# A factorization-machine tower on one core: the order-zero Gram matrices computed in 64x64 tiles, two samples at a time

## What is computed

```
h = e                                  # layer 0
for i, (W, b) in enumerate(layers):    # W0, W1, W2 with 128 outputs each
    nxt = einsum('bjk,bzk,ojz->bok', h, e, W.reshape(O, Hj, 32)) + b
    h, o = nxt[:, :64], nxt[:, 64:]    # the last layer gives all 128 to o
z = sum over k of all the o            # [512, 256]
y = relu(relu([z, dense_ctx] @ W_top1 + b_top1) @ W_top2 + b_top2) @ W_top3
```

## Time and profile before

| | us |
|---|---|
| median of three runs (lowest, highest) | 696.14 (693.29, 696.73) |
| the profiled execution's own time | 695.17 |
| its span, first to last instruction | 693.4 |
| TensorE matmul busy | 652.9 (94%) |
| VectorE busy | 483.7 (70%) |
| ScalarE busy | 215.4 (31%) |
| GpSimd busy | 129.6 (19%) |

### The profile page before, as it was taken

How to read it: one execution, slowest core, us unless ns; L and a number is a source line. 1 busy time by engine, 2 the same in 40 slices (tenths; PEclk the granted TensorE clock), 3 DMA queues, 4 the chain that set the end, 5 groups by cost and what they waited for, 6 DMA issues and landing times.

```text
span 693.4 us, 32990 instructions
## 1 busy us (share of the span) xinstructions
PE 652.9 (94%) x15000; PEld 513.3 (74%) x15000; DVE 483.7 (70%) x488; ACT 215.4 (31%) x354; POOL 129.6 (19%) x137
## 2 busy tenths in 40 slices
PE   5745999999999999999999999999999999999798
PEld 5734767777778777877878787878788887888563
DVE  4238878888888888888888888888888888820000
ACT  2331333333334333433333333333333333331002
POOL 7755134454445444000000000000000000000000
PEclk9976999999999999999999999999999999999889
DMA  5100011111111111000000000000000000020000
GB/s 174 29 19 17 15 20 23 23 24 23 23 23 21 20 20 23 9 10 9 8 8 8 8 8 8 8 8 8 8 8 8 8 8 8 8 70 9 4 1 0
DMA packets 13036, 12.64 MB, mean 18 GB/s; under 512 B 5649, under 2 KB 10305, under 8 KB 12754
## 3 DMA queue, kind: packets, MB, share of 16 engines
q1 hardware_dynamic: 8818, 7.99, 4.5%
q0 software_dynamic: 4192, 4.25, 3.1%
HBM read 8.03 MB, written 0.00 MB: 12 GB/s over the span
## 4 chain that ended last, share of the span: by engine, by line
PE 89%; POOL 5%; issue 3%; DVE 2%; DMA 1%; ACT 0%; ACTq 0%; DVEq 0%; POOLq 0%
PE psX L315 20%; PE psT L369 19%; PE psT L353 8%; PE psT L393 8%; PE psT L379 7%; PE psT L356 5%; PE psX L324 5%; POOL G_sb L219 5%; PE psX L353 4%; PE psX L356 4%; PE psX L443 2%; PE psX L332 1%; DVE PT L692 1%; PE psT L469 1%; PE psX L458 1%
## 5 line engine op out<-in xcount | busy, mean ns | idle before, releaser
L373 PE MATMUL psT<-T_sb,W1d 64*64 64x256 f32 x1024 | 234.3, 379 | 0.0
L369 PE MATMUL psT<-T_sb,W1d 64*64 64x256 f32 x1024 | 234.3, 379 | 0.0
L379 PE MATMUL psT<-T_sb,W1d 64*64 64x256 f32 (+3 forms) x2048 | 205.3, 300 | 0.0
L656 DVE TENSOR_TENSOR prod<-X 128x1024 f32 (+4 forms) x202 | 170.7, 913 | 18.4 <-PE psT L356 18.2
L692 DVE STREAM_TRANSPOSE PT<-prod 128x4608 f32<-128x4608 f32 x32 | 159.0, 4968 | 0.0
L369 PEld LDWEIGHTS psT<-T_sb,W1d 64*64 64x64 f32 x1024 | 131.3, 133 | 29.4 <-issue 17.1
L315 PE MATMUL psX<-PT,W0T 32*64 32x256 f32 x4608 | 137.0, 380 | 10.1 <-DVE PT L692 9.1
L393 PE MATMUL psT<-T_sb,W1d 64*64 64x64 f32 (+2 forms) x1536 | 141.7, 270 | 0.0
L315 PEld LDWEIGHTS psX<-PT,W0T 32*64 32x64 f32 x4608 | 117.2, 133 | 32.1 <-issue 27.1
L373 PEld LDWEIGHTS psT<-T_sb,W1d 64*64 64x64 f32 x1024 | 131.3, 133 | 0.0
L379 PEld LDWEIGHTS psT<-T_sb,W1d 64*64 64x64 f32 x2048 | 123.6, 133 | 0.8
(11 more groups left out here) (74 smaller groups left out, 570.1 us busy)
## 6 DMA issues: line engine op xcount, KB each, us to landing
X<-T_sb SPq DMA_DIRECT2D x64, 64.0 KB, 1.9
G_sb<-in_L_rec_W SPq DMA_DIRECT2D x2, 1024.0 KB, 6.7
E_q<-in_tbl,ids_g POOLq DMA_INDIRECT x96
prod<-in_W_top SPq DMA_DIRECT2D x2, 512.0 KB, 4.2
G_sb<-in_L_rec_W SPq DMA_DIRECT2D x1, 512.0 KB
G_sb<-in_tbl,ids POOLq DMA_INDIRECT x32, 2.4
zb<-in_L_rec_b SPq DMA_DIRECT2D x4, 0.2 KB
ids_g<-in_ids POOLq DMA_DIRECT2D x3, 16.0 KB, 2.0
```

Of the source, the lines that this page charges most:

```text
L369: mm(psT[low, 0, 0:HF * SMP], W1d[low, HF + k, :], cross.rearrange("p v (z y) s -> p v z y s", y=HF)[:, :, :, k, :], start=start, stop=sto ...
L373: mm(psT[high, 0, 0:HF * SMP], W1d[low, k, :], T_flat[low, SMP * row:SMP * (row + HF)], start=start, stop=stop, tile_position=(0, C))
L379: last = mm(out[:, SMP * 4 * a:], W1d[high, HF * v + k, :], T_flat[high, SMP * (row + 4 * a):SMP * (row + HF)], start=start, stop=stop and ...
L656: return tt(out, x[:, :, z0:z0 + nz].unsqueeze(3).broadcast_to(shape), x[:, :, y0:y0 + ny].unsqueeze(2).broadcast_to(shape), ALU.mult)
```

## The change

G0 of two neighbouring tiles is computed by one matmul in a 64x64 tile of the array. `fields` holds, for each pair of tiles, a one, 32 fields of the first, 32 fields of the second, and a one: 66 columns (`GRAM`). 64 of them are the weights, all 66 are moved, so the 64x66 result has the two Gram matrices on its diagonal blocks, the sums beside them, and two cross blocks that nobody reads. There are 8 such matmuls in a step in place of 16.

In `kept` each sample has 34 columns (`NS`), 33 of them written: a sample of an even tile has its ones in column 0, one of an odd tile in column 33, and the fields are columns 1 to 32. The column that is not written is set to zero once at the start. Since where a 32-partition quarter's columns lie depends on the quarter being even or odd, `g0_copy` becomes four copies, one for each quarter of the partitions, each as long in the free dimension as the one before. `z0` and `z2` read `kept` at the shifted columns. `T_BANKS` exchanges the banks of tiles 2 and 3, and `t_matmuls` has its waits in the order that follows from it.

```diff
-NS = NF + 1
+NS = NF + 2
+GRAM = 2 * NF + 2
+ONES = (0, NF + 1)
...
-        fields = sb("fields", [P, 2, TILES, NS])
+        fields = sb("fields", [P, 2, TILES // 2, GRAM])
...
-        T_BANKS = [psT[:, 2:4], psX[:, 0:2], psX[:, 2:4], psT[:, 0:2], psT[:, 2:4], psX[:, 0:2], psT[:, 0:2], psT[:, 2:4]]
+        T_BANKS = [psT[:, 2:4], psX[:, 0:2], psT[:, 0:2], psX[:, 2:4], psT[:, 2:4], psX[:, 0:2], psT[:, 0:2], psT[:, 2:4]]
...
             def g0_matmuls(m, e):
-                for t in range(TILES):
+                for pair in range(TILES // 2):
+                    q, g = pair // 2, pair % 2
                     for h in range(2):
-                        x = fields[C * h:C * h + C, e, t, :]
-                        j, q = t % 4, t // 4
-                        last = mm(psX[Q * j:Q * j + Q, 2 + h, NS * q:NS * (q + 1)], x[:, 0:NF], x,
-                                  start=True, stop=True, tile_position=(C * h, Q * j))
+                        x = fields[C * h:C * h + C, e, pair, :]
+                        last = mm(psX[C * g:C * g + C, 2 + h, GRAM * q:GRAM * (q + 1)], x[:, 1:1 + 2 * NF], x,
+                                  start=True, stop=True, tile_position=(C * h, C * g))
                 last.then_inc(g0_ready, 1)
 
             def t_matmuls(n, e):
                 for t in range(TILES):
                     if t == 2:
+                        pe.wait_ge(g2_copied, n + 1)
+                    if t == 3:
                         pe.wait_ge(g0_evac, n + 1)
-                    if t == 3:
-                        pe.wait_ge(g2_copied, n + 1)
                     if t == 4:
                         pe.wait_ge(t_by_act, NA * n + 1)
-                    if t in (5, 6):
-                        pe.wait_ge(t_by_dve, ND * n + t - 4)
-                    if t == 7:
-                        pe.wait_ge(t_by_act, NA * n + 3)
+                    if t == 5:
+                        pe.wait_ge(t_by_dve, ND * n + 1)
+                    if t in (6, 7):
+                        pe.wait_ge(t_by_act, NA * n + t - 4)
...
-                              kept[:, n0:n0 + STEPS // 2, 4 * NF:4 * NS].rearrange("p n (q h) -> p n q h", h=2),
+                              kept[:, n0:n0 + STEPS // 2, 4 * ONES[j % 2]:4 * ONES[j % 2] + 4]
+                              .rearrange("p n (q h) -> p n q h", h=2),
...
-                c = 4 * y
+                c = 4 * (1 + y)
...
             def g0_copy(m):
                 act.wait_ge(g0_ready, m + 1)
-                copy(kept[:, bass.ds(m, 1), :].rearrange("p n (c q h) -> p (n h) q c", q=2, h=2),
-                     psX[:, 2:4, 0:2 * NS].rearrange("p h (q c) -> p h q c", q=2)).then_inc(g0_evac, 1)
+                for j in range(4):
+                    r, i = slice(Q * j, Q * j + Q), j % 2
+                    last = copy(kept[r, bass.ds(m, 1), 4 * i:4 * (i + NF + 1)].rearrange("p n (c q h) -> p (n h) q c", q=2, h=2),
+                                psX[r, 2:4, 0:2 * GRAM].rearrange("p h (q c) -> p h q c", q=2)[:, :, :, (NF + 1) * i:(NF + 1) * (i + 1)])
+                last.then_inc(g0_evac, 1)
...
+            for c in ONES:
+                nc.vector.memset(kept[:, :, 4 * c:4 * c + 4], 0.0)
             nc.vector.memset(V_T[:, :, :], 0.0).then_inc(zeroed, 1)
-            nc.vector.memset(fields[:, :, :, NF:NS], 1.0)
+            nc.vector.memset(fields[:, :, :, 0:GRAM:GRAM - 1], 1.0)
...
             def x_of(e, first_tile):
-                cp(fields[:, e, :, 0:NF], X_fields[:, bass.ds(first_tile, TILES), :])
+                cp(fields[:, e, :, 1:1 + 2 * NF],
+                   X_fields[:, bass.ds(first_tile, TILES), :].rearrange("p (pair i) f -> p pair (i f)", i=2))
```

## The result

The changed kernel takes 712.56 us (median of four runs, 709.79 to 714.34) against 696.43 for the kernel before (median of four, one run more than in the table ahead), a ratio of 1.0241 (95% interval 1.0205 to 1.0278). It is slower by 16.1 us; the forecast was 713.5. The profiled execution took 711.53, 16.4 more than the one before.

A forecast was written before the change was run, and what follows sets the result against it. TensorE, busy for 94% of the span, was taken as the bound, with ScalarE's copies on the edge of its critical path; 31 x 0.56 = +17.4 on 695.17 gives 712.5, plus 0.97 to the median, 713.5; range 693 to 722.

The forecast's parts named there:

- the middle: ScalarE, start of the first small copy: between 0.62 as now and 0.70, when G2's copy has ended; 0.66 taken.
- The rule on the partitions: ScalarE's four copies: runs whose partitions change don't overlap, so 0.417 each, 1.67 for the four.
- The saving: G0's matmuls on TensorE: 16 record pairs in place of 32 save 0.14 of 0.29, swallowed by the chain over ScalarE.
- The last step: TensorE from tile 7 to H: H follows 0.64 behind, at 5.50 against 4.94, +0.56 us in each step.
- rival A: ScalarE's four copies overlap at 0.21 each; H comes 0.32 a step earlier, -10 us, 686; chance 0.16.
- The sign that the old copy overlapped both its neighbours: ScalarE's old G0 copy: starts 0.51 after G2's copy, which lasts 0.59; taken as speaking for overlapping copies.
- The estimate of 0.20: ScalarE, a copy of 132: 186 ns + 0.833 ns an element, back-to-back ones overlapping by about 93 ns.
- B: ScalarE's four copies are short, 0.265 each, but don't overlap; -0.05 a step, -1.6 us, 694.5; chance 0.14.
- C: ScalarE's four copies are dearer, 0.48 each; H at 5.76, +0.82 a step, +25, 721.5; chance 0.08.

The follow-up runs named there:

- the other layout: The changed kernel with kept laid out so that each of the four copies writes runs of 33 neighbouring elements: 697.26 us, ratio 1.0035.

## Why the prediction was right

**The bound and the chain.** The prediction put the change on the chain from G2's copy over G0's copies, tile 0's copy, tile 4 and tile 7 to H, and took +0.56 us a step; it was +0.53. Its terms in a step of the kind that it read, from the start of G2's copy (0.11 less than in the prediction, which counted from G0):

| | predicted | measured |
|---|---|---|
| from one quarter copy to the next | 0.417 | 0.41 |
| tile 0's copy starts | 2.22 | 2.13 |
| tile 4 released | 3.04 | 2.95 |
| tile 7 released | 4.71 | 4.63 |
| H's weights start | 5.39 | 5.43 |

The 0.09 by which tile 0's copy is early has two sources: the first small copy overlaps G2's fully (0.48; the prediction took the middle, 0.55), and each small one is 0.392 long, not 0.405. The rule on the partitions was read from three runs of copies and held; the four on the same partitions show it directly. So the mechanism was right: the copies do not overlap, each at the length that the pattern in kept gives it, and tiles 4 and 7 wait for it.

**G0.** The saving was put at 0.14 and is 0.22 to 0.24. It was said to be swallowed, and at the release of tile 7 it is, to 0.01, in the steps without lookups; in most of those with lookups 0.2 arrives. The gap of 0.28 in the weight loads before G0 is gone.

**What failed.** The last step, "H follows 0.64 behind" tile 7's matmuls, and that a step grows by as much as H's start moves. It gave H's start in the shorter steps within 0.04, but the kernel with the new order alone has those matmuls 0.19 earlier and H's end, without lookups, where it was. H's weights start 0.60 later than before in the shorter steps and 0.67 in the longer ones, while these steps grow by 0.48 and 0.58: some 0.1 comes back in H and behind it. The prediction has neither, nor the two kinds of steps. H's end keeps to 5.0 to 5.3 behind the release of tile 7 in the undisturbed steps of every kernel in the loop without lookups (read from 350 us on), and what it is in between depends on TensorE's own path through the loop. So the present stall of tile 6, which rival A counted as 0.18 to be won, could not be won there by the order alone. These errors are small beside the copies, and that they nearly cancel, with the 0.08 by which tile 7's release is early, is luck: the 0.03 between forecast and measurement is better than the terms.

**The rivals.** A (the copies overlap) did not happen; but its price of a copy is real where the partitions stay (0.23), and its gain of 10 us is about the 9 that one wide copy gave. The sign that the old copy overlapped both its neighbours was half misread: in the earlier trace rows it ends at 516.08, before tile 0's copy starts. The estimate of 0.20 from the Trainium skill (ScalarE: Activation LUTs, What ACT_TABLE_LOAD costs) that stood beside it was not met: 132 elements took 0.392 in steps of 16 bytes and 0.263 in runs of neighbours, against the 0.296 of its formula, and did not overlap. B (short copies that don't overlap) had its price in the other layout, and its time nearly (2 us more than before, not 2 less). C was not near.

**What stays open.** Why H and the stretch behind it take up to 0.2 longer in the loop without lookups when G0 has its sixteen matmuls (up to 4.44, and 8.36, in place of 4.27 and 8.31). It is not the 64x32 tiles alone: in the loop with lookups H takes 4.27 with them too, and in the undisturbed steps of the unrolled loop 4.25. Something in how the loop's instructions come fits that, but no run changed their number alone. Nor was it tried how much of G0's 0.22 is the eight matmuls fewer and how much the tile shape that no longer changes.

## What to carry to other kernels

Before splitting an evacuation by partitions, price it as the full length of every piece: pieces that start on other partitions queued end to end here (0.41 each), while the same pieces on the same partitions overlapped (0.23), and one copy over everything, even of twice the columns, was the cheapest (0.28 to the next). An engine that is busy for a third of the time can still be the bound in the one stretch where another waits for its buffers; put the work into it there with the fewest instructions, and the untidy part where it is idle anyway. And when a stall is removed, look whether the wait behind it ends any earlier: here, without lookups, it did not. When two kernels have steps of two kinds, compare like with like: a difference of 0.14 between two steps can be the branch and not the change.

## What the runs showed of the hardware that was not expected

- ScalarE holds back a copy whose first partition differs from the last one's; a copy of fewer partitions with the same first one overlaps (0.48 after the start of a 0.58 copy; the four copies 0.41 apart from first partitions that differ, 0.23 from the same).
- Elements written 16 bytes apart made a ScalarE copy of 132 elements last 0.392 in place of 0.263.
- A branch on TensorE that goes one way in every second step shows: H's weights started 0.93 to 0.98 after tile 7's release in one kind of step without lookups and 0.75 to 0.87 in the other, in all the kernels with the branch, and 0.86 in every undisturbed one of the kernel before unrolled.
- The same loop, made twice as long, cost 5 to 8 us in 8 of 31 steps of the profiled execution, and showed itself in the instruction queue's packets (22 to 103), while its undisturbed steps without lookups were 0.19 faster.
